# Attention's block ends: turn and first output product ahead of the scores, norms and flips behind them

## The reference, cut to what matters

```python
q = (layernorm(x) @ wq)      # 32 heads of 128, rope
k = (ctx @ wk); v = (ctx @ wv)   # 8 heads, four query heads share one
...
scores = jnp.einsum('bhgqd,bhkd->bhgqk', qg, k) / scale
w = jax.nn.softmax(masked, axis=-1)
out = jnp.einsum('bhgqk,bhkd->bhgqd', w, v)
x = x + jnp.tanh(g_xattn[1]) * (out @ wo)
```

## Time and profile before

| | |
|---|---|
| median of 3 runs | 3185.18 us (3184.72 to 3187.27) |
| the profiled execution | 3188.17 us |
| its span, first to last instruction | 3186.3 us |
| mean granted TensorE clock | 0.988 |
| PE busy | 3094.2 us, 97% |
| DVE busy | 1944.9 us, 61% |
| ACT busy | 1135.5 us, 36% |
| POOL busy | 701.2 us, 22% |

### The profile page before, as it was taken

One profiled execution on the slowest core, in us unless ns is written; L12 is line 12 of the kernel. 1 busy time (PEld: TensorE's weight loads), 2 busy tenths in 40 slices (PEclk: granted clock), 3 DMA queues, 4 the chain that ended last, 5 costly groups with the idle time before them and its releaser, 6 DMA issues.

```text
span 3186.3 us, 42408 instructions
## 1 busy us (share of the span) xinstructions
PE 3094.2 (97%) x15136; PEld 2582.5 (81%) x15136; DVE 1944.9 (61%) x4651; ACT 1135.5 (36%) x2381; POOL 701.2 (22%) x576
## 2 busy tenths in 40 slices
PE   8999999998899899999999999999999999999999
PEld 7888778787678778888788888788888788888887
DVE  4333478777453577778666667666667666666532
ACT  4111466664122244444333333333333333333320
POOL 2422388884212123333100000000000000000131
PEclk9999999999899999999999999999999999999999
DMA  7332422113352577777564454465454454543621
GB/s 239 126 126 93 154 55 73 57 44 136 123 194 103 179 224 232 242 256 241 179 241 162 159 190 162 144 213 165 164 182 162 153 203 168 172 159 120 258 92 55
DMA packets 232877, 509.61 MB, mean 160 GB/s; under 512 B 23180, under 2 KB 58124, under 8 KB 232668
## 3 DMA queue, kind: packets, MB, share of 16 engines
q1 hardware_dynamic: 231516, 504.14, 46.5%
q10 hardware_dynamic: 1152, 2.75, 0.3%
HBM read 364.23 MB, written 142.61 MB: 159 GB/s over the span
## 4 chain that ended last, share of the span: by engine, by line
PE 66%; DVE 3%; ACT 1%; POOL 0%; issue 0%; DMA 0%; DVEq 0%; ACTq 0%; POOLq 0%; SPq 0%
PE PB L208 54%; PE PB L769 8%; PE PB L1301 3%; PE PB L740 1%; PE PB L1215 0%; DVE at_st L213 0%; ACT at_ss L1282 0%; DVE f0xt L793 0%; DVE at_hl L196 0%; ACT at_xr L219 0%; DVE f1st L213 0%; DVE at_ss L1276 0%; POOL at_wol L196 0%; POOL at_st L217 0%; DVE at_xt L1337 0%
## 5 line engine op out<-in xcount | busy, mean ns | idle before, releaser
L208 PE MATMUL PB<-at_woh,at_ah 128*128 128x512 f32 x1024 | 412.6, 403 | 3.6 <-POOL at_wol L196 1.9
L208 PE MATMUL PB<-at_hh,at_wqh 128*128 128x512 f32 x1024 | 401.4, 392 | 0.2 <-DVE at_hl L196 0.2
L208 PE MATMUL PB<-at_woh,at_al 128*128 128x512 f32 x1024 | 401.5, 392 | 0.0
L208 PE MATMUL PB<-at_hl,at_wqh 128*128 128x512 f32 x1024 | 401.1, 392 | 0.0
L208 PE MATMUL PB<-at_wol,at_ah 128*128 128x512 f32 x1024 | 401.1, 392 | 0.0
L208 PE MATMUL PB<-at_hh,at_wql 128*128 128x512 f32 x1024 | 400.3, 391 | 0.0
L1282 ACT ACTIVATE at_ss<-at_ss,at_sm,at_bs 128x256 f32<-128x256 f32 x512 | 301.4, 590 | 266.8 <-DVE at_sm L1280 266.8
L1249 DVE TENSOR_TENSOR at_t<-PB,at_rt 128x512 f32<-128x512 f32 x128 | 88.5, 691 | 436.1 <-PE PB L208 436.1
L1337 DVE SCALAR_TENSOR_TENSOR at_xt<-PB,gt,at_xt 128x512 f32<-128x512 f32 x256 | 190.6, 746 | 115.9 <-PE PB L208 115.9
L193 ACT ACTIVATE at_ah<-PB 128x512 fp32r<-128x512 f32 x128 | 76.7, 599 | 483.1 <-PE PB L208 483.1
L208 PEld LDWEIGHTS PB<-at_woh,at_al 128*128 128x128 f32 x1024 | 193.5, 189 | 41.4
(11 more groups left out here) (274 smaller groups left out, 7175.4 us busy)
## 6 DMA issues: line engine op xcount, KB each, us to landing
at_wqh<-wqd SPq DMA_DIRECT2D x96, 512.0 KB, 3.6
at_wql<-wqd SPq DMA_DIRECT2D x96, 512.0 KB, 4.5
at_woh<-wod SPq DMA_DIRECT2D x48, 1024.0 KB, 5.1
at_wol<-wod SPq DMA_DIRECT2D x48, 1024.0 KB, 7.6
at_rawq<-in_wq SPq DMA_DIRECT2D x32, 512.0 KB, 5.0
wqd<-at_wqh SPq DMA_DIRECT2D x32, 512.0 KB, 6.5
wqd<-at_wql SPq DMA_DIRECT2D x32, 512.0 KB, 7.5
at_rawo<-in_wo SPq DMA_DIRECT2D x32, 512.0 KB, 6.6
```

The costliest lines, as they stand in the source:

```text
L208: e.matmul(o, a, b, start=i == 0, stop=last), *(waits if i == 0 else ()), *w, mark=last)
```

## The change

In periods 30 and 31 of the first three blocks, and in period 0 of the three blocks that follow, `turn(u-1)` and the first `output` now come ahead of `scores(u)`. The norms of tiles 2 and 3 are issued right behind the scores of w = 29 and w = 30. In w = 31 (and 30) `values(u-1)` comes ahead of the second output; the flips of tile 3 stay behind the turn but are now also behind the scores and the values; the flips of tiles 1 and 2 come behind `values` at the end of their periods. The next block's first two projections come behind the second output of w = 31. `split_ahead` becomes two functions, so that the split of wo's part comes ahead of those projections and the load of wq behind them.

```diff
-            def split_ahead(u):
+            def split_wo_ahead(u):
                 n, hf, jj = half_of(u)
                 if 0 <= n < G:
                     split_wo(n, hf, jj)
+
+            def split_wq_ahead(u):
                 if u + 4 < H:
                     split_wq(u + 4)
                 elif u + 4 < NU and u % 32 != 30:
...
+                last = w == 31 and more
+                new = w == 0 and 0 < u < NU
+                first = late or last or new
+                if first:
+                    turn(u - 1)
+                    output(n - 1, 2 * k)
                 if u < NU:
                     scores(u)
-                last = w == 31 and more
+                if more and w in (29, 30):
+                    nq[w - 27] = norm(qn + 1, w - 27)
                 rest = project(u + 2) if u + 2 < NU and not late and not last else None
...
-                if 1 <= u <= NU:
+                if late or last:
+                    values(u - 1)
+                if last:
+                    flip(qn + 1, 3, 0, nq[3])
+                    flip(qn + 1, 3, 1, nq[3])
+                if 1 <= u <= NU and not first:
                     turn(u - 1)
                 if rest and u >= 4:
                     rest()
-                if last:
-                    flip(qn + 1, 3, 0, nq[3])
-                    flip(qn + 1, 3, 1, nq[3])
+                if n and not first:
+                    output(n - 1, 2 * k)
+                if more and w == 29:
+                    flip(qn + 1, 0, 0, nq[0])
+                    flip(qn + 1, 0, 1, nq[0])
+                    fetch_x(qn + 1, 3)
+                if u == NU:
+                    values(u - 1)
                 if n:
-                    output(n - 1, 2 * k)
+                    output(n - 1, 2 * k + 1)
+                if 4 <= u < NU:
+                    weigh(u)
+                if 4 <= u < NU and not late and not last:
+                    values(u - 1)
+                if more and w == 29:
+                    flip(qn + 1, 1, 0, nq[1])
+                    flip(qn + 1, 1, 1, nq[1])
+                if late:
+                    flip(qn + 1, 2, 0, nq[2])
+                    flip(qn + 1, 2, 1, nq[2])
+                split_wo_ahead(u)
                 if last:
                     project(u + 1)()
                     load_wq(u + 3)
                     project(u + 2)()
...
+                split_wq_ahead(u)
                 if more and w == 27:
                     nq = {t: norm(qn + 1, t) for t in range(2)}
-                if more and w in (29, 30):
-                    nq[w - 27] = norm(qn + 1, w - 27)
```

## The result

The changed kernel takes 3190.15 us (median of 20 runs, 3187.28 to 3194.44), the kernel before 3184.82 beside it (20 runs, 3183.26 to 3190.32): 1.0016 times as long, 95% interval 1.001 to 1.0022. That is 5.3 us more; forecast were 4.3 more, within the 0.2% that were to be called no change. The second comparison, with the last group of experiments, gave 3192.26 against 3185.27, 1.0021 (1.0012 to 1.003).

The account below looks back on a forecast made before the run. The prediction took PE, busy for 97% of the span, as the bound, with some 20 us of waiting and the slow clock behind it to change. Waits -2.9 plus clock +7.2 gave +4.3 us, about 3189.4; range 3181.2 to 3194.7.

Parts of the forecast that it names:

- Waits alone: Three block ends, PE's waits without added clock loss: 1.1, 1.1 and 0.7 us less, together -2.9 us.
- Period 29: Second half of tile 1's flip waits 1.15 us for the bank of values(28), against 1.07 before; nothing won.
- Period 30: Second half of tile 2's flip waits 2.15 us for the bank of values(29); before, values(29) waited 1.62.
- Period 31, turn: turn(30), now first in its period, waits a new 1.0 us for its normalised operand.
- Tile 3: Second half of tile 3's flip waits 3.2 us for the bank of values(30); before, 3.21 for the norm.
- scores(32): Second half of scores(32) waits 0.35 us for head 33's query, between bounds of 0 and 0.5.
- First end: output(4) in the first block end waits 3.45 us for POOL's subtraction of wo's part, against 1.9 before.
- The clock: Slow stretches after PE's waits in the block ends: 4.5 of seven places at 1.6 us, +7.2 us.
- the pairs: In each end the waits 2.15 + 1.0 us, at tile 2's flip and turn(30), as one possible slow-clock place.
- the clock holds: Rival: slow clock at two places or fewer in the block ends, -2.9 to +0.5 us; chance 0.15.
- Slower, all seven places: Rival: slow clock at all seven places of the block ends, 1.7 us each, 3194.2 us; chance 0.15.
- Faster: Rival: banks aren't the limit, flips in the block ends stop waiting; -17.6 us, 3167.6; chance 0.08.

Follow-up runs that it names:

- e3_fill: The changed kernel with 35 unread matmuls in its first block end and 21 in the others, put where PE waits; 3185.53 us, 0.9997 of the kernel before.
- e5_bank: The changed kernel with the second half of tile 3's flip written to bank 0 instead of the alternating bank; 3180.75 us, 0.9982 of the kernel before.
- e2_flips_first: The changed kernel with tile 3's two flips moved ahead of scores(31), right behind output(6); 3177.61 us, 0.9974 of the kernel before.
- e4_zero_old: The changed kernel without the lead of turn and output in period w = 0, scores(32) first again; 3204.63 us, 1.0058 of the kernel before.
- e10_changed_again: The changed kernel once more, unedited, against new runs of the kernel before; 3192.26 us, 1.0021 of the kernel before.
- e9_norms_late: The changed kernel with the norms of tiles 2 and 3 back at the ends of w = 29 and 30; 3204.23 us, 1.006 of the kernel before.
- e6_no_lead: The changed kernel with turn and first output behind the scores again in w = 30 and 31; 3190.59 us, 1.0016 of the kernel before.
- e8_order2: The same work as the kernel before in another order over periods 29, 30, 31 and 0, with half flips spread out; 3156.78 us, 0.9906 of it.
- e1_norms_only: The kernel before with only the norms of tiles 2 and 3 moved right behind the scores of w = 29 and 30; 3181.04 us, 0.9984 of it.

## Why the prediction was right

The forecast was +4.3 us (3189.5 by its own sum, put down as 3189.4), waits traded for others and a loss to the clock; measured +5.3, and +7.0 the second time. The waits came out where and nearly as long as laid out; the clock's term was right in size, but in part by luck.

- **Waits alone, -2.9.** e3_fill shows the order at full clock: 75.08, 71.60 and 71.58, laid out as 74.85, 71.4 and 71.4. Against before it is -2.3; both sums set the new order at full clock against before with its own slow stretches.
- **Period 29, 1.15.** Measured 1.07, as long as the wait there before; nothing won, as said. The early norm(2) cost nothing that shows.
- **Period 30, 2.15.** Measured 1.92. **Period 31, turn 1.0.** One idle of 0.41 is listed, the rest lies between its transposes: the group takes 1.55 us at full clock in e3_fill, 1.03 in a normal period. That makes 0.9.
- **Tile 3, 3.2.** Measured 3.02. That it is the bank, and the copy behind the exponentials, is shown by e5_bank and e2_flips_first from two sides.
- **scores(32), 0.35.** Measured 0.21. e4_zero_old shows how near the edge it is: 3.8 without the cover.
- **First end, 3.45 for POOL.** Measured 3.28. (21.9 less 18.35 is 3.55, not 3.45; it changes nothing.)
- **The clock, +7.2** by 4.5 places at 1.6 us. The profiled execution had five places, one of them of double length, so six stretches and 8.3 us, 1.4 for each. The number of stretches was taken too low and the price of one too high, and the two partly cancel; the 1.7 as upper bound of a place was wrong too, as the 6.8 us stretch in the earlier trace rows could have told. In the next profiled execution it was seven places, eight stretches and 11.5 us. And my choice of places was poor. I held the four single long waits for the surest and the pairs for doubtful. All three pairs fell, the 3.28 and one of the three waits at tile 3 did not, and in the next execution all seven did.

Of the rivals, "the clock holds" didn't happen; e3_fill shows what it would have been. What spoke for it, that no single wait but in the first end is longer than before, didn't fit my own layout, which has 2.15 in place of 1.62 and a new 1.0, and just this pair fell every time. "Slower, all seven places" happened in the profiled execution of e10_changed_again. The Trainium skill ("TensorE: Matmul & The Clock Gate", section "A second HAM failure mode: psum-queue depth-cycling"), by which frequent short idles between groups of matmuls that cycle through the banks make the clock swing, was nearer the mark than I allowed. This case agrees in part: 1.92 + 0.41 brought the clock down in every end of both profiled executions, while the bank wait of 1.07 at tile 1 never did. "Faster" needed the banks not to be the limit; e5_bank shows the limit, and that lifting it at one flip gives back some 11 us against the changed kernel. The rule that the rest of the forecast stood on, that one must count what is queued on ACT ahead of a split, gave the waits of the later ends within 0.4 us in the experiments, but for two flips in third ends with the clock down: tile 2's in e9_norms_late (2.0 expected, none there) and tile 3's in e6_no_lead (1.2 expected, 0.7 there).

## What to carry to other kernels

An early input doesn't help a stage whose buffer is late: before moving work up, list for each moved group the bank it takes and everything that is queued on the releasing engine ahead of the copy that frees it. Put burst work (here four exponentials, 2.34 us) behind the small copies that others wait for, as e2_flips_first does, or let one PE group pass in between; e8_order2 does it with half flips. And price PE's waits with the clock behind them: here each slow stretch of 3.4 us cost some 1.4 us, on top of the 2.3 us of waits at tile 2 and turn(30) that came before it.

## What the runs showed that I had not expected

- Matmuls that nobody reads made a kernel faster. 77 of them, in rows of 3.43 us once and of 2.10 and 3.23 us in each end, 19.4 us of PE time, stood where PE waited anyway, and none of the six slow stretches of the block ends was left. The mean granted clock was 0.991 to 0.993 in all 11 runs, against 0.988 to 0.992 in the 20 of the changed kernel.
- The clock's fall isn't a property of the wait alone. In the same program the wait of 3.28 to 3.29 us at output(4) passed at full clock once and brought 1.2 GHz the next time. The shorter waits were the surer ones: 1.92 + 0.41 at tile 2 and turn(30), with transposes around them, had a slow stretch in all 15 ends of the five profiled executions with waits of this length (changed kernel twice, e2_flips_first, e4_zero_old, e5_bank). In two of the ends it began ahead of turn(30)'s wait and left only 0.17 and 0.34 of it. The 3.02 at tile 3 had one only in 5 of 9 ends (changed kernel twice, e4_zero_old). No run separates why. In e1_norms_only the clock was at its lower level for 10.2 us of the first end and for 3.4 us of each later one.
- The later ends can be packed without a gap: 63.42 us, PE busy 63.42.
